# New instruction orders for five engines, eight warm pairs instead of ten, and the last half added and stored in two pieces

## The chip, the cores and the metric

One core of one Trainium2 chip runs the whole program. The metric is the device time of an execution in microseconds. The engines are TensorE (PE), VectorE (DVE), ScalarE (ACT), GpSimd (POOL) and SyncE (SP, which here only issues DMAs). SBUF is the on-chip memory that engines and DMA share; PSUM holds what PE writes.

## What is computed

Two layers of self-attention over the 32 x 32 pixels of 4 images with 128 channels, the second on the output of the first:

```python
n = h * w
xf = x.reshape(b, c, n)
q = jnp.einsum('rc,bcn->brn', Wq, xf) + bq[None, :, None]
k = jnp.einsum('rc,bcn->brn', Wk, xf) + bk[None, :, None]
v = jnp.einsum('oc,bcn->bon', Wv, xf) + bv[None, :, None]
energy = jnp.einsum('bri,brj->bij', q, k)
attn = jax.nn.softmax(energy, axis=2)
out = jnp.einsum('bcj,bij->bci', v, attn).reshape(b, c, h, w)
return gamma * out + x
```

Here b = 4, c = 128, n = 1024 and q, k have 16 rows. The second layer has other weights and the same form.

## The kernel before

There are 8 stages: 0 to 3 are the images in layer 0, 4 to 7 the same images in layer 1, so stage s + 4 needs the output x of stage s. Each stage works on 8 row tiles of 128 pixels. PSUM has a ring of three buffers [128 x 1024] and `out_psum` for the output. In a stage, by the names that the orders use:

- `QX`, `QK`: PE projects q and k in two steps (L630 to L643). `evac` (ACT) then `mask`, `stack` (POOL) do this for stage 1, `mask`, `stack` on DVE for stages 2 to 7 (L525 to L539): they add the bias and round to fp32r with a remainder, packed into `qk`. For stage 0 it is `raw` (L618): PE writes ring 0 and ring 1, ACT evacuates `qk_raw` and DVE `swapped_raw` in halves of 512 columns, and POOL stacks qk of stage 0 from `qk_raw` (L422 to L428). Energies of stage 0 use `qk_raw` and `swapped_raw`; tile i needs both halves of `qk_raw`, and only the first half of `swapped_raw` if i < 4 (L665, L666).
- `swap`: SP issues two DMAs that exchange the halves of `qk` into `qk_swapped` (L320 to L324).
- `E.s.i.r`: PE makes the energies of tile i in ring buffer r. `max` (DVE, L561) takes the negative row maximum, `sum` (ACT, L469) the row sums of exp, `log` (ACT) their logarithm.
- `parts` (POOL, L391 to L396), `shift` (PE), `rows` (DVE, L572) and `place` (SP, L326 to L336) bring maximum and logarithm as two extra rows into `qk`, so that
- `ET.s.k.r`: the transposed energies come out already shifted, and `attn` (ACT, L484) is exp of them. Before `attn` of stage s may overwrite tile k, the `lo` of tile k of the stage before must be done (or, for tiles 0 and 7, its product).
- `hi.s.k` and `lo.s.k`: tiles 1 to 6 of attn are cut in two fp32r numbers, `attn_hi` = rounded attn and `attn_lo` = attn - attn_hi. Tiles 0 and 7 are multiplied as fp32 and not cut. A `hi` is done by POOL (L359) or ACT (L490), a `lo` by POOL (L364) or DVE (L558). `v32` (DVE, L548), `v_hi` (POOL L370 or ACT L495) and `v_lo` (POOL L376 or DVE L553) do the same for v.
- `PH`: products of attn_hi with v_hi and v_lo (L741). `PV`: the product of attn_lo with v_hi, or for tiles 0 and 7 attn with v in fp32 (L747 to L752). They accumulate in `out_psum`.
- `finish.s.h` (DVE, L575): x plus gamma times the product, for one half of 512 columns. In stages 6 and 7 (`WHOLE`) a half is complete in one bank and takes one instruction (L586); elsewhere two. `store` (SP, L338) writes a half of layer 1's output to DRAM.

What runs when is written out by hand: `PE_ORDER`, `ACT_ORDER`, `DVE_ORDER`, `POOL_ORDER` and `SP_ORDER` (L51 to L113) list the pieces of each engine, with the loops over them at L589, L761 and their like. An engine takes its list strictly in order, and waits on semaphores for what each piece reads or overwrites. Which engine has a `hi`, `lo`, `v_hi` or `v_lo` is decided by the list in which it stands. `warm.0.n` in PE's order is n pairs of matmuls on a tile of zeros (`keep_warm`, L754), and `WARM_UP` = 10 such pairs run ahead of everything, as soon as POOL has cleared the zeros (L759, L760). Their results are not used.

At the start SP issues all loads: `weights` first (L310), then the two halves of x of stage 0 (L313), and the rest.

Of the kernel before, what the change touches and what calls it, by code (L numbers as in the profile page):

```python
# [832 lines left out]
```

## Time and profile before

| | us |
|---|---|
| median of 3 runs | 193.52 |
| lowest and highest of them | 192.95, 193.8 |
| the profiled execution | 193.06 |
| its span, from the first to the last instruction | 191.3 |
| busy in the span: PE, POOL, ACT | 179.1, 156.9, 155.5 |
| busy in the span: DVE | 145.7 |

The profile is one execution taken by the hardware profiler. A share of busy time over the whole span is a mean over a start, a long middle part and a tail, which have different limits, so the same numbers are better read by stretch. The chain that ended last is followed back from the last instruction to what released each one; it tells which engine was waited for, and in which part. Of a wait for several semaphores the profile names the one that came last.

### The profile page before, as it was taken

The numbers are of one execution on the slowest core, as the hardware profiler recorded it, in microseconds if no ns is written. First come the engines' busy times: TensorE is split into PE (matmuls) and PEld (weight loads), VectorE is DVE, ScalarE is ACT, GpSimd is POOL, SyncE is SP. The second block draws the span as 40 slices with busy tenths as digits, with TensorE's granted clock in tenths as the row PEclk, the third lists the DMA queues.
The fourth block names the chain that finished last, engine by engine and source line by source line (L and its number), as shares of the span: only waits on it lengthen the run. The fifth ranks groups of instructions, "written<-read, shape, count | busy, mean of one in ns | idle before, by whom it ended". The sixth has DMA issues, their size and how long they took to land.

```text
span 191.3 us, 3482 instructions
## 1 busy us (share of the span) xinstructions
PE 179.1 (94%) x1282; PEld 123.1 (64%) x1282; DVE 145.7 (76%) x137; ACT 155.5 (81%) x223; POOL 156.9 (82%) x120
## 2 busy tenths in 40 slices
...
GB/s 155 345 104 0 215 9 42 69 3 3 2 113 0 5 111 3 0 3 3 110 3 0 3 55 58 2 3 107 61 55 7 55 0 58 3 0 55 55 55 55
DMA packets 3890, 9.51 MB, mean 50 GB/s; under 512 B 548, under 2 KB 932, under 8 KB 3876
## 3 DMA queue, kind: packets, MB, share of 16 engines
...
## 4 chain that ended last, share of the span: by engine, by line
PE 34%; POOL 31%; ACT 15%; issue 10%; DMA 4%; DVE 4%; SPq 1%; POOLq 0%; DVEq 0%; ACTq 0%
POOL attn_lo L364 14%; PE out_psum L720 10%; POOL attn_hi L359 9%; ACT ring L472 8%; PE out_psum L722 7%; ACT attn L484 4%; DMA qk_swapped<-qk 4%; PE ring L671 3%; PE ring L697 3%; PE out_psum L756 3%; PE ring L642 2%; DVE neg_max L563 2%; PE ring L624 2%; PE ring L657 2%; ACT attn_hi L490 2%
## 5 line engine op out<-in xcount | busy, mean ns | idle before, releaser
L364 POOL TENSOR_TENSOR attn_lo<-attn,attn_hi 128x1024 fp32r<-128x1024 f32 x37 | 90.4, 2455 | 1.8 <-ACT attn_hi L490 1.3
L563 DVE TENSOR_REDUCE neg_max<-ring 128x1 f32<-128x1024 f32 x64 | 75.6, 1219 | 15.7 <-PE ring L673 15.3
L472 ACT ACTIVATE ring<-ring,neg_max 128x1024 f32<-128x1024 f32 x64 | 69.6, 1087 | 9.9 <-DVE neg_max L563 9.3
L484 ACT ACTIVATE attn<-ring 128x1024 f32<-128x1024 f32 x64 | 63.3, 1024 | 9.8 <-DVE attn_lo L558 5.6
L359 POOL TENSOR_SCALAR attn_hi<-attn 128x1024 fp32r<-128x1024 f32 x35 | 39.2, 1134 | 5.5 <-ACT attn L484 5.4
L699 PE MATMUL ring<-qk_swapped,qk 64*128 64x512 f32 x64 | 29.0, 478 | 0.0
L697 PE MATMUL ring<-qk,qk_swapped 64*128 64x512 f32 x64 | 28.5, 468 | 0.3
L671 PE MATMUL ring<-qk_swapped,qk 64*128 64x512 f32 x56 | 25.1, 452 | 3.4 <-ACT attn L484 1.7
L673 PE MATMUL ring<-qk,qk_swapped 64*128 64x512 f32 x56 | 25.7, 461 | 0.0
L558 DVE TENSOR_TENSOR attn_lo<-attn,attn_hi 128x1024 fp32r<-128x1024 f32 x11 | 19.4, 1778 | 5.5 <-POOL attn_hi L359 4.7
L723 PE MATMUL out_psum<-attn_hi,v_hi 64*128 64x512 f32 x72 | 23.0, 399 | 0.0
L722 PE MATMUL out_psum<-attn_hi,v_hi 64*128 64x512 f32 x72 | 23.0, 398 | 0.0
L723 PE MATMUL out_psum<-attn,v 64*128 64x512 f32 x48 | 22.6, 590 | 0.0
L722 PE MATMUL out_psum<-attn,v 64*128 64x512 f32 x48 | 22.6, 590 | 0.0
L722 PE MATMUL out_psum<-attn_hi,v_lo 64*128 64x512 f32 x72 | 22.2, 388 | 0.0
L723 PE MATMUL out_psum<-attn_hi,v_lo 64*128 64x512 f32 x72 | 22.2, 388 | 0.0
L722 PE MATMUL out_psum<-attn_lo,v_hi 64*128 64x512 f32 x72 | 20.9, 392 | 0.1
L723 PE MATMUL out_psum<-attn_lo,v_hi 64*128 64x512 f32 x72 | 20.9, 392 | 0.0
L697 PEld LDWEIGHTS ring<-qk,qk_swapped 64*128 64x128 f32 x64 | 11.5, 184 | 10.9 <-issue 9.9
L657 PEld LDWEIGHTS ring<-late,x_all 64*128 64x128 f32 x256 | 16.6, 187 | 2.5 <-issue 1.7
L671 PEld LDWEIGHTS ring<-qk_swapped,qk 64*128 64x128 f32 x56 | 10.3, 184 | 12.3 <-issue 10.3
L657 PE MATMUL ring<-late,x_all 64*128 64x128 f32 x256 | 17.6, 275 | 0.2 <-ACT ring L472 0.2
...
## 6 DMA issues: line engine op xcount, KB each, us to landing
qk_swapped<-qk SPq DMA_DIRECT2D x16, 256.0 KB, 3.7
out_dram<-x_all SPq DMA_DIRECT2D x8, 256.0 KB, 2.0
...
x_all<-x_in SPq DMA_DIRECT2D x2, 256.0 KB, 3.0
...
weights<-weights_in SPq DMA_DIRECT2D x1, 131.0 KB, 2.2
qk<-shift_rows SPq DMA_DIRECT2D x7, 8.0 KB
```

What stands on the lines that cost most here:

```text
L359: nc.gpsimd.tensor_scalar(attn_hi[:, k - 1], attn[:, k], 1.0, 0.0, ALU.mult, ALU.add).then_inc(cut_made["hi", "gpsimd"], 1)
L364: nc.gpsimd.tensor_tensor(attn_lo[:, k - 1], attn[:, k], attn_hi[:, k - 1].bitcast(fp32), ALU.subtract).then_inc(cut_made["lo", "gpsimd"], 1)
L472: nc.scalar.activation(e[:], e[:], ACT.Exp, bias=neg_max[s][:, i:i + 1], accum_out=row_sum[s][:, i:i + 1]).then_inc(sum_made, 1)
L484: nc.scalar.activation(attn[:, k], ring_tile("ET", s, k)[:].rearrange("p (a n) -> p a n", a=2), ACT.Exp).then_inc(attn_made, 1)
L563: nc.vector.tensor_reduce(neg_max[s][:, i:i + 1], ring_tile("E", s, i)[:], axis=AX.X, op=ALU.max, negate=True).then_inc(max_made, 1)
L657: last = nc.tensor.matmul(to[:, chunk], x_all[rows, s, chunk], late[rows, WV + layer(s)], start=step == 0 and j == 0, stop=step == 1 and j ...
L671: nc.tensor.matmul(to[:, 0:HALF], q_over_k[0:64, rows], k_over_q[0:64, 0:HALF], start=True, stop=True)
L673: nc.tensor.matmul(to[:, HALF:N], k_over_q[64:128, rows], q_over_k[64:128, HALF:N], start=True, stop=True).then_inc(e_mm, 1)
L697: nc.tensor.matmul(to[:, 0:HALF], k_over_q[0:64, first], q_over_k[0:64, part], start=True, stop=not added(s, h))
L699: last = nc.tensor.matmul(to[:, HALF:N], q_over_k[64:128, second], k_over_q[64:128, part], start=True, stop=not added(s, h))
L722: nc.tensor.matmul(out_psum[:, 0:HALF], v[0:64], a[0:64], start=start, stop=stop)
L723: last = nc.tensor.matmul(out_psum[:, HALF:N], v[64:128], a[64:128], start=start, stop=stop)
```

## The change

1. All five orders are new. The same pieces are computed, 64 `E`, 64 `ET`, 48 `PH`, 64 `PV` and so on. What changes hands: POOL has 33 `lo` instead of 37 and DVE 15 instead of 11; POOL has 34 `hi` instead of 35 and ACT 14 instead of 13; POOL has 4 `v_lo` instead of 5 and DVE 4 instead of 3; POOL has 5 `v_hi` instead of 3 and ACT 3 instead of 5. DVE's `lo` are now 0, 1, 3, 0, 1, 1, 5 and 4 in stages 0 to 7, where they were 0, 1, 1, 0, 1, 1, 4 and 3. POOL's `hi` are now 5, 5, 5, 4, 5, 4, 3 and 3, where they were 5, 5, 5, 4, 3, 6, 4 and 3. POOL's `v_hi` are now of stages 0, 1, 3, 4 and 6, where they were of 1, 3 and 5; its `v_lo` of 0, 1, 2 and 7, where they were of 0, 1, 2, 4 and 5.
2. `WARM_UP` is 8. The pairs within PE's order are 19 instead of 18.
3. `weights` is loaded by ACT's queue, ahead of ACT's table load; SP starts with x.
4. SP swaps stage 0 before stage 1.
5. The last `finish` (7.1) is two instructions of 256 columns with a semaphore of their own, and its store two DMAs.

```diff
-HALF = N // 2
+HALF, QUARTER = N // 2, N // 4
...
-WARM_UP = 10
+WARM_UP = 8
...
 PE_ORDER = """
-raw.0.0.0 raw.0.1.1 E.0.6.2 QX.1.0.0 E.0.0.1 QK.1.0.0 E.0.7.2 warm.0.2 E.0.4.0 E.0.2.1 E.0.1.2 warm.0.2 E.0.3.0
...
+raw.0.0.0 raw.0.1.1 warm.0.1 E.0.1.2 QX.1.0.0 E.0.2.1 QK.1.0.0 E.0.0.2 warm.0.2 E.0.7.0 E.0.3.1 E.0.5.2 warm.0.2
...
 SP_ORDER = """
-swap.1.0 swap.0.0 place.0.0 swap.2.0 place.0.1 place.1.1 swap.3.0 place.2.1 swap.4.0 place.3.1 swap.5.0 place.4.1
+swap.0.0 swap.1.0 place.0.0 swap.2.0 place.0.1 place.1.1 swap.3.0 place.2.1 swap.4.0 place.3.1 swap.5.0 place.4.1
...
+LAST = [use[1:3] for use in DVE_USES if use[0] == "finish"][-1]
...
         @block.sync
         def _(sp):
-            sp.dma_start(weights[:], weights_in).then_inc(weights_loaded, 16)
...
             def store(s, h):
+                if (s, h) == LAST:
+                    for q in range(2):
+                        part = slice(h * HALF + q * QUARTER, h * HALF + (q + 1) * QUARTER)
+                        sp.wait_ge(last_made, q + 1)
+                        sp.dma_start(out[s - B, :, part], x_all[:, s, part]).then_inc(stored, 16)
+                    return
...
-            sp.wait_ge(stored, 32 * B)
+            sp.wait_ge(stored, 32 * B + 16)
...
         @block.scalar
         def _(act):
+            act.dma_start(weights[:], weights_in).then_inc(weights_loaded, 16)
             act.preload_act_table_set("natural_log_exp_and_others")
...
+                if (s, h) == LAST:
+                    for q in range(2):
+                        part = slice(h * HALF + q * QUARTER, h * HALF + (q + 1) * QUARTER)
+                        nc.vector.scalar_tensor_tensor(out=x_all[:, s, part], in0=out_psum[:, part], scalar=gamma,
+                                                       in1=x_all[:, s, part], op0=ALU.mult, op1=ALU.add
+                                                       ).then_inc(last_made, 1)
+                    return
```

How the orders come out on the engines is shown at three places; the line numbers of the changed kernel are up to 17 higher. First PE, just behind the last matmul of the raw projection. The two instructions into a ring buffer from `swapped_raw` and `qk_raw` are one energy tile, those from `x_all` and `weights` the steps QX and QK of stage 1. Before:

```order
L624 MATMUL ring1<-x_all,weights 128x512
L671 MATMUL ring2<-swapped_raw,qk_raw 128x512
L673 MATMUL ring2<-qk_raw,swapped_raw 128x512
L642 MATMUL ring0<-x_all,weights 128x512 x2
L671 MATMUL ring1<-swapped_raw,qk_raw 128x512
L673 MATMUL ring1<-qk_raw,swapped_raw 128x512
```

After:

```order
L641 MATMUL ring1<-x_all,weights 128x512
L773 MATMUL out_psum<-zeros 128x512
L774 MATMUL out_psum<-zeros 128x512
L688 MATMUL ring2<-swapped_raw,qk_raw 128x512
L690 MATMUL ring2<-qk_raw,swapped_raw 128x512
L659 MATMUL ring0<-x_all,weights 128x512 x2
L688 MATMUL ring1<-swapped_raw,qk_raw 128x512
```

A warm pair has come in, and the sequence of forms is otherwise the same; the tiles are E.0.1 and E.0.2 where they were E.0.6 and E.0.0.

Second DVE, from `v32` of stage 3 to the end of stage 2's first `finish`. Before:

```order
L548 TENSOR_TENSOR v32_1<-ring2,late 128x1024
L558 TENSOR_TENSOR attn_lo<-attn,attn_hi 128x1024
L572 CAST shift_rows1<-ring0 16x128
L563 TENSOR_REDUCE neg_max4<-ring1 128x1
L563 TENSOR_REDUCE neg_max4<-ring0 128x1
L563 TENSOR_REDUCE neg_max4<-ring2 128x1
L563 TENSOR_REDUCE neg_max4<-ring1 128x1
L581 SCALAR_TENSOR_TENSOR x_all<-out_psum,weights,x_all 128x512
```

After:

```order
L558 TENSOR_TENSOR v32_1<-ring1,late 128x1024
L568 TENSOR_TENSOR attn_lo<-attn,attn_hi 128x1024
L582 CAST shift_rows1<-ring2 16x128
L568 TENSOR_TENSOR attn_lo<-attn,attn_hi 128x1024
L573 TENSOR_REDUCE neg_max4<-ring2 128x1
L540 TENSOR_SCALAR masked_hi<-ring0,weights 128x1024
L573 TENSOR_REDUCE neg_max4<-ring1 128x1
L547 SCALAR_TENSOR_TENSOR qk2<-ring0,weights,masked_hi 128x1024
L568 TENSOR_TENSOR attn_lo<-attn,attn_hi 128x1024
L598 SCALAR_TENSOR_TENSOR x_all<-out_psum,weights,x_all 128x512
```

DVE has three `lo` here where it had one, and mask and stack of stage 5 stand ahead of the `finish` instead of behind it, with fewer maxima.

Third POOL, from the last `parts` to its end. Before:

```order
L391 TENSOR_TENSOR shift7<-neg_max7,log_sum7 128x8
L394 TENSOR_SCALAR shift_parts7<-shift7 128x8
L396 TENSOR_TENSOR shift_parts7<-shift7,shift_parts7 128x8
L364 TENSOR_TENSOR attn_lo<-attn,attn_hi 128x1024
L359 TENSOR_SCALAR attn_hi<-attn 128x1024
L364 TENSOR_TENSOR attn_lo<-attn,attn_hi 128x1024
L359 TENSOR_SCALAR attn_hi<-attn 128x1024
L364 TENSOR_TENSOR attn_lo<-attn,attn_hi 128x1024
```

After:

```order
L400 TENSOR_TENSOR shift7<-neg_max7,log_sum7 128x8
L403 TENSOR_SCALAR shift_parts7<-shift7 128x8
L405 TENSOR_TENSOR shift_parts7<-shift7,shift_parts7 128x8
L385 TENSOR_TENSOR v_lo1<-v32_1,v_hi1 128x768
L368 TENSOR_SCALAR attn_hi<-attn 128x1024 x3
L373 TENSOR_TENSOR attn_lo<-attn,attn_hi 128x1024
L368 TENSOR_SCALAR attn_hi<-attn 128x1024
L373 TENSOR_TENSOR attn_lo<-attn,attn_hi 128x1024
```

Behind the last `parts` POOL had five `lo` and four `hi`; now it has `v_lo` of stage 7, four `hi` and two `lo`. `hi.6.3`, which stood second there, is in ACT's order now.

## Rows read from the trace of the kernel before

**Rows 1.** Busy us and instructions by stretch; then clock, DMA share, GB/s.

```profile
core 0: us, PE busy (x) PEld busy (x) DVE busy (x) ACT busy (x) POOL busy (x), PEclk, DMA share, GB/s
12.00:23.00 11.00, 10.31 (x61) 4.17 (x58) 8.80 (x8) 9.84 (x17) 4.46 (x5) 1.00 0.30 73
40.00:140.00 100.00, 96.80 (x787) 72.25 (x785) 85.85 (x84) 94.56 (x138) 98.26 (x70) 1.00 0.12 31
...
158.70:188.10 29.40, 28.13 (x112) 17.82 (x110) 18.48 (x15) 16.61 (x20) 20.72 (x13) 1.00 0.10 36
```

**Rows 2.** The chain that ended last, from the page, by engine.

```profile
PE 34%; POOL 31%; ACT 15%; issue 10%; DMA 4%; DVE 4%; SPq 1%; POOLq 0%; DVEq 0%; ACTq 0%
```

**Rows 3.** Timeline of the start: start us, us, instruction, [idle before <- releaser].

```profile
1.19 0.89 SPq L313 DMA_DIRECT2D x_all<-x_in  x2
...
1.31 0.60 PE L756 MATMUL out_psum<-zeros 64*128 64x512 bf16 x1 [1.31 <-POOL zeros L354]
...
4.70 0.54 PE L756 MATMUL out_psum<-zeros 64*128 64x512 bf16 x1
...
5.08 0.38 PE L756 MATMUL out_psum<-zeros 64*128 64x512 bf16 x1
...
5.38 3.70 PE L624 MATMUL ring<-x_all,weights 128*128 128x512 f32 x8
...
8.27 0.69 ACT L458 ACTIVATE qk_raw<-ring,weights 128x512 f32<-128x512 f32 x1 [0.96 <-PE ring L624]
...
10.02 0.66 PE L671 MATMUL ring<-swapped_raw,qk_raw 64*128 64x512 f32 x1 [0.94 <-DVE swapped_raw L519]
...
14.73 0.38 PE L756 MATMUL out_psum<-zeros 64*128 64x512 bf16 x1
...
14.95 0.38 PE L756 MATMUL out_psum<-zeros 64*128 64x512 bf16 x1
```

**Rows 4.** DMA issues, from the page: count, KB each, median us to landing.

```profile
out_dram<-x_all SPq DMA_DIRECT2D x8, 256.0 KB, 2.0
...
x_all<-x_in SPq DMA_DIRECT2D x2, 256.0 KB, 3.0
...
weights<-weights_in SPq DMA_DIRECT2D x1, 131.0 KB, 2.2
```

**Rows 5.** Two pieces of the chain that ended last: start us, us.

```profile
13.76 1.12 ACT unstacked L466
...
23.02 0.49 PE ring L671
```

**Rows 6.** Group of v_lo on POOL: busy us, mean ns, idle before.

```profile
L376 POOL TENSOR_TENSOR v_lo<-v,v_hi 128x768 fp32r<-128x768 f32 x5 | 9.1, 1826 | 0.0
```

**Rows 7.** Timeline rows of POOL and DVE in the middle.

```profile
82.74 2.37 POOL L364 TENSOR_TENSOR attn_lo<-attn,attn_hi 128x1024 fp32r<-128x1024 f32 x1
85.08 0.84 POOL L370 TENSOR_SCALAR v_hi<-v 128x768 fp32r<-128x768 f32 x1
...
123.70 1.43 DVE L558 TENSOR_TENSOR attn_lo<-attn,attn_hi 128x1024 fp32r<-128x1024 f32 x1
...
124.01 1.81 POOL L370 TENSOR_SCALAR v_hi<-v 128x768 fp32r<-128x768 f32 x1
```

**Rows 8.** Timeline rows from 160 to 170 us.

```profile
160.21 1.21 DVE L558 TENSOR_TENSOR attn_lo<-attn,attn_hi 128x1024 fp32r<-128x1024 f32 x1
...
162.66 2.84 DVE L558 TENSOR_TENSOR attn_lo<-attn,attn_hi 128x1024 fp32r<-128x1024 f32 x1
...
164.38 2.02 POOL L359 TENSOR_SCALAR attn_hi<-attn 128x1024 fp32r<-128x1024 f32 x1
...
166.55 0.70 PE L720 MATMUL out_psum<-attn_hi,v_hi 128*128 128x512 f32 x2 [1.20 <-POOL attn_hi L359]
...
169.93 1.03 ACT L484 ACTIVATE attn<-ring 128x1024 f32<-128x1024 f32 x1 [5.56 <-DVE attn_lo L558]
```

**Rows 9.** Timeline rows of the end.

```profile
188.07 0.75 DVE L586 SCALAR_TENSOR_TENSOR x_all<-out_psum,weights,x_all 128x512 f32<-128x512 f32 x1 [4.14 <-PE out_psum L720]
...
188.85 0.33 SPq L341 DMA_DIRECT2D out_dram<-x_all  x1
```

More of the change, by code:

```diff
@@ L73 @@
+PV.6.2 PH.6.5 PH.6.4 ET.7.0.0 ET.7.4.1 ET.7.1.2 PV.6.4 PH.7.3 PV.6.5 ET.7.6.1 ET.7.5.0 PV.7.0 PH.7.1 PV.7.3 PH.7.2
+PH.7.5 PV.7.1 PV.7.2 PH.7.4 PH.7.6 PV.7.5 PV.7.4 PV.7.6 PV.7.7
 """
 ACT_ORDER = """
[L75 to L77 removed]
@@ L83 @@
[L83 to L86 removed]
+sum.0.1 evac.1.0 sum.0.2 sum.0.0 sum.0.7 sum.0.3 sum.0.5 sum.0.4 log.0.0 sum.0.6 sum.1.0 sum.1.6 sum.1.7 log.0.1
@@ L87 @@
+attn.7.4 attn.7.0 attn.7.1 attn.7.5 hi.7.5 hi.7.4 attn.7.6 hi.7.6
 """
 DVE_ORDER = """
-max.0.6 max.0.0 max.0.7 max.0.4 max.0.2 max.0.1 max.0.3 max.0.5 max.1.4 rows.0.0 v32.0.0 max.1.7 max.1.6 mask.2.0
-stack.2.0 max.1.5 max.1.0 max.1.2 rows.0.1 max.1.3 max.1.1 max.2.4 max.2.7 max.2.1 rows.1.1 v32.1.0 finish.0.0
-max.2.3 max.2.0 mask.3.0 stack.3.0 max.2.6 max.2.2 max.2.5 finish.0.1 v32.2.0 lo.1.1 max.3.0 rows.2.1 max.3.1
-max.3.2 mask.4.0 stack.4.0 finish.1.0 max.3.6 max.3.5 max.3.4 max.3.3 max.3.7 max.4.4 finish.1.1 v32.3.0 lo.2.2
@@ new lines @@
+lo.2.3 max.4.0 mask.5.0 max.4.6 stack.5.0 lo.2.6 finish.2.0 max.4.3 v_lo.3.0 max.4.4 max.4.1 max.4.7 max.5.5
+finish.2.1 max.4.5 v32.4.0 max.5.1 max.5.4 rows.4.1 max.5.7 max.5.3 finish.3.0 mask.6.0 stack.6.0 v_lo.4.0 max.5.6
+max.5.0 max.5.2 max.6.1 finish.3.1 lo.4.1 v32.5.0 rows.5.1 max.6.3 max.6.2 max.6.0 v_lo.5.0 max.6.6 finish.4.0
+mask.7.0 stack.7.0 max.6.7 max.6.5 max.6.4 finish.4.1 rows.6.1 v32.6.0 max.7.6 max.7.0 max.7.4 max.7.2 finish.5.0
+max.7.5 max.7.7 max.7.1 lo.6.2 lo.5.6 v_lo.6.0 finish.5.1 max.7.3 v32.7.0 lo.6.6 rows.7.1 lo.6.3 lo.6.5 lo.6.4
@@ L99 @@
+finish.6.0 finish.6.1 lo.7.1 lo.7.2 lo.7.5 lo.7.4 finish.7.0 finish.7.1
 """
 POOL_ORDER = """
-mask.1.0 stack.1.0 parts.0.0 parts.0.1 v_lo.0.0 hi.0.2 hi.0.3 hi.0.1 lo.0.2 lo.0.3 lo.0.1 parts.1.1 hi.0.6 lo.0.6
-v_hi.1.0 hi.0.4 v_lo.1.0 lo.0.5 lo.0.4 hi.1.2 hi.1.1 hi.1.3 lo.1.2 parts.2.1 lo.1.3 hi.1.6 hi.1.5 lo.1.6 lo.1.5
-hi.2.1 v_lo.2.0 lo.1.4 hi.2.3 hi.2.2 lo.2.3 parts.3.1 hi.2.4 lo.2.1 v_hi.3.0 lo.2.6 hi.2.5 lo.2.4 lo.2.5 hi.3.3
-hi.3.1 hi.3.2 lo.3.2 lo.3.3 parts.4.1 lo.3.1 hi.3.4 lo.3.4 lo.3.6 lo.3.5 hi.4.3 hi.4.2 v_lo.4.0 lo.4.3 hi.4.1
```

80 lines of the change are left out of this document (39 added, 41 removed).

## The prediction

> **What bounds the kernel now.** I read the busy time by stretch first. From 40 to 140 us GpSimd (POOL) is busy 98.26 of 100 us, the tensor engine (PE) 96.80, ScalarE (ACT) 94.56 and VectorE (DVE) 85.85 [rows 1]. So there is no single slow engine: POOL has 1.7 us free, ACT 5.4, DVE 14.2, and the PE figure has to be read with care, since the ends of matmuls are modelled. Then the chain that ended last: PE 34% and POOL 31% of it, with ACT at 15% [rows 2]. In order of time it is the start-up through the first stages (to 23 us), then POOL, then PE. For the last 29.4 us, 158.7 to 188.1, PE is busy 28.13 [rows 1], nearly all products of the last two stages. Three regimes follow, and I cost the change in each: a serial start, a stretch where POOL has hardly a gap, and a tail where PE works off its queue.
>
> I use E for energies, ET for transposed energies, hi and lo for the two parts of an attention tile, v_hi and v_lo for those of v, as the orders do.
>
> **The start.** Ten warm pairs are issued before the raw projection. The last pairs start at 4.27, 4.70 and 5.08 us and the projection at 5.38 [rows 3]. From 1.31 to 4.70 there are eight pairs, one in 0.42 us; between two pairs at 14.73 and 14.95 it is 0.22 us. 512 columns in 0.42 and in 0.22 us are the 1.2 and the 2.4 GHz level. The pair at 4.70 takes 0.38, between the two: if x us of it are at the low level, 1.2x + 2.4(0.38 - x) = 0.512 thousand columns gives x = 0.33, so the clock rose at about 5.03 us. The engine had then been working without a break since 1.31 us. Two pairs fewer let the projection begin at 4.70, of which 0.33 us pass at half pace: 0.68 - 0.17 = **0.5 us earlier**. That needs the first half of x by 4.70. Its transfer is now issued at 1.19 us and that form takes 3.0 us to land [rows 3, 4], so about 4.2; with weights moved to ACT's queue it is issued 0.45 us sooner. No cost there: the work of ACT that follows waits for the projection. The bound on the other side: if the clock did not rise until the projection was over, its 8 rows in 3.70 us [rows 3] would take about 3.4 us more. I take no such delay, because PE has no idle gap there with 8 pairs either.
>
> Next, the first energies. Now E.0.6 is first; it reads rows of the second half of swapped_raw, and PE idles 0.94 us for it until 10.02 [rows 3]. Afterwards E.0.1 is first: it needs both halves of qk_raw but only the first half of swapped_raw. qk_raw's second half is written from 8.27 for 0.69 us, so to 8.96 [rows 3]. E.0.1 can start at about 9.03 rather than 10.02, the extra warm pair (0.22 us) fitting in the gap. E.0.2 then needs ring 1, free at 9.87, and E.0.1 with QX.1 keep PE busy beyond that. So QX.1 and QK.1, which stand in the same places, come **1.0 us earlier**. These 1.0 and 0.5 go on whole through the chain evac, mask and stack, swap, first E of stage 1 (evac at 13.76, the E at 23.02) [rows 5], since each step there starts when the one before it ends. SP now issues swap.0 before swap.1; POOL makes qk of stage 0 before that of stage 1, so it delays nothing and takes a transfer out of the chain's way: a gain if anything, taken as 0. One more warm pair in all within the order, 0.22 us, falls among waits: 0. **Start: -1.5 us.**
>
> **The middle.** POOL's run without a gap begins with hi.0.2. Counted in the orders from there to the end of stage 5: POOL gives up two lo (stage 2), v_lo.4 and v_lo.5; the hi of stage 4 and 5 exchange two for two with ACT; v_hi.4 comes and v_hi.5 goes. A lo is 2.37, a v_lo 1.83 on average [rows 6, 7]: 2 x 2.37 + 2 x 1.83 = 8.4 us off. v_hi.0, now POOL's, lies before the run, where POOL is busy 4.46 of 11 us [rows 1]: nothing. parts.0.1, which was before the run, is now inside: +0.8.
>
> But the work goes to DVE, and that is not free for POOL. At 123.70 DVE starts a lo; the v_hi that POOL starts at 124.01 takes 1.81 us, where the same form takes 0.84 when DVE is not at such an instruction (85.08) [rows 7]. So POOL stood about 1.0 us for a DVE instruction with two SBUF operands. Four such more: +3.9. The Trainium skill has this as a rule (SBUF — State Buffer, "SBUF: two separate sides"): the two engines share one pair of ports, and whichever starts first keeps it for its whole instruction. The trace agrees, with 1.81 against 0.84. Another place (Perfetto Trace Analysis, "Optimizing Scalar/DVE Operations") says that moving operations between these two "might not help". By the rows it helps by 2.37 - 1.0 = 1.4 for a lo; by that rule it would be 0, which is the first rival below.
>
> POOL's stretch thus falls by 8.4 - 0.8 - 3.9 = 3.7 us. That is an upper bound on what arrives at the end: ACT has only 5.4 us free in the same 100 and PE 3.2 [rows 1], each partly start-up of instructions, and an order is followed strictly, so what POOL wins is partly handed to waits for ACT or PE. The lower bound is 0, with a loss possible (third rival). DVE has the room: 4 x 1.2 = 4.8 us more against 14.2 free. I choose **-2.2 us**, some 60%, nearer to the upper end because POOL's row of the middle shows that these orders can keep it fed while ACT is at 95%.
>
> **The tail.** In the last two stages POOL has one lo fewer in each, v_lo.7 and v_hi.6 more; DVE one more lo in each, without v_lo.7; ACT v_hi.6 less and one hi more in stage 6. The products are the same, and PE sets the end. So only waits of PE count. The one of size is at 166.55, 1.20 us for hi.6.3 on POOL, which took 2.02 us because DVE's lo.6.6 (162.66, itself 2.84 for want of the port) ran beside it; and DVE's lo.6.3 after it kept ACT waiting 5.56 us, until 169.93 [rows 8]. In the new order hi.6.3 is ACT's, behind attn.6.4, and no port can hold it. The 1.20 can vanish; the five lo of stage 6 on DVE can bring a wait like it, since each can lose 1.6 us (2.84 against the 1.21 at 160.21 [rows 8]) to a POOL instruction. Ends: -1.2 and +1; taken **-0.6 us**.
>
> **The last half.** Now one instruction of 0.75 us from 188.07, a store issued at 188.85, landed about 2.0 us later [rows 9]. Per 512 columns more DVE needs about 0.5 us (1.21 for 1024 [rows 8] against 0.75), so a piece of 256 columns is 0.5 us and the second ends 0.4 later: 0.15 us later than now. The second store's 0.33 us of issue is free to go at once, as the first was issued 0.4 before. It carries half the bytes. One bound is the landing of 131 KB of weights, 2.2 us; the other the gap between those and a half of x of twice the size, 3.0 - 2.2 = 0.8 us [rows 4]. So the end moves between +0.15 + 0.2 = +0.35 and 0.15 - 0.8 = -0.65. The nearest row is the store's own, alone on the queues where the loads are not, so I take 1.75 instead of 2.0 for it: **-0.1 us**.
>
> **Sum.** -1.5 - 2.2 - 0.6 - 0.1 = -4.4 us. The profiled execution took 193.06 us, of which 191.3 is span; that gives 188.7. The median of the runs shown is 0.46 higher, which would give 189.1. I put down 188.9.
>
> **Rivals.**
> First, the moves between POOL and DVE bring nothing: DVE's lock costs as much as POOL sheds, or PE and ACT, 3 and 5 us behind POOL, become the bound at once. Then the start and the last half stay: 193.06 - 1.6 = 191.5. For it: three engines above 94%. Against it: 1.0 us of blocking for 2.37 of work.
> Second, all of it arrives: -1.5 - 3.7 - 1.2 - 0.25 = -6.65, so 186.4. For it: every stretch is then limited by what was shortened. Against: ACT would have to run at over 98%.
> Third, slower: DVE becomes the engine waited for. Five more of its instructions want the port while POOL holds it; at the 1.6 us that lo.6.6 lost, that is 8.2 us of waiting, and row maxima stand behind them, for which ACT waits and with ACT the ring and PE. At half of that, +4.1 with the middle's gain gone: 193.06 - 1.6 + 4.1 = 195.6. It turns the sign once more than 1.6 of the 8.2 us reach ACT. Against it: DVE's 14.2 us of room, which lie between these maxima. A small variant is the clock: risen only after the projection, 3.4 us lost, with the gains about 192.
> Fourth, the change does less than it says: the order's pairs of lo and POOL instructions fall elsewhere in time than planned, and waits merely move. That ends at the first rival's time.
>
> **How the numbers follow.** Forecast (187.3 to 190.7) 0.50; first and fourth rival (190.7 to 192.6) 0.23; second (below 187.3) 0.15; third (above 192.6) 0.12. The range runs from 186.2, which leaves out the better half of the second, to 192.5, which takes in the first. A measurement of this kernel can tell about 0.5%, 1 us. Faster by more than that, below 192.55: 0.50 + 0.20 + 0.14 = 0.84; within 0.5%: 0.07, from the first rival's edge and the mildest third; slower 0.09.
>
> **What would show it.** The raw projection begins near 4.7 us and its matmuls keep 0.43 us a row after 5.0; the first E stands near 8.5 and the first E of stage 1 near 21.5. If these are late, the start is wrong. POOL's busy time over the run should fall by 7 or so with some gaps for ACT or PE; if the fall is there but the end of stage 5 is not earlier by more than the start gave, the first rival holds. DVE's lo and v_lo tell the third: a mean above 2 us, and ACT idle for neg_max over 10 us. PE's wait of 1.20 before PH.6.3 should be gone, and from the start of DVE's last step to the end of the span 2.9 to 3.3 us should pass (3.2 now).

## The result: 2.4% slower, and the profile after

| | before | changed |
|---|---|---|
| median of the runs of this comparison, us | 193.24 (4 runs, 192.73 to 193.80) | 198.13 (4 runs, 196.58 to 198.66) |
| ratio, with its 95% interval | | 1.0237 [1.0198, 1.0275] |
| profiled execution, us | 193.06 | 196.58 |
| its span | 191.3 | 194.5 |
| busy PE, POOL, ACT, DVE | 179.1, 156.9, 155.5, 145.7 | 180.7, 145.3, 156.9, 151.8 |

Medians here and below are of all executions of a kernel, and the ratios leave out the slow ones, more than 1.5% above the kernel's fastest (one of lo26, one of clear_new, two of slow_three), so differences between experiments are taken from the ratios (0.01 is 1.9 us).

The forecast was 188.9 us with a range to 192.5. The time came out 5.6 us above that range, on the other side of the kernel before. The moves themselves arrived: POOL is busy 11.6 us less, DVE 6.1 more. What they were to buy did not.

The busy time by stretch of the changed kernel, to be held against [rows 1] (the second stretch is the tail again, 3.1 us later, since the end lies later):

```profile
core 0: us, PE busy (x) PEld busy (x) DVE busy (x) ACT busy (x) POOL busy (x), PEclk, DMA share, GB/s
40.00:140.00 100.00, 93.91 (x735) 71.63 (x734) 89.78 (x84) 89.85 (x126) 90.45 (x67) 0.98 0.11 29
161.80:191.30 29.50, 28.85 (x128) 18.64 (x124) 15.10 (x17) 18.76 (x22) 14.13 (x11) 1.00 0.10 37
```

From 40 to 140 us PE works off 735 instructions where it worked off 787, ACT runs 126 instructions instead of 138. POOL, which had 1.7 us free, has 9.6. DVE alone is busier, 89.78 instead of 85.85. In the tail PE stands idle for 0.65 us of 29.5, half of the 1.27 before.

The chain that ended last, by engine, from the page, against [rows 2]:

```profile
PE 51%; POOL 21%; DVE 13%; issue 8%; ACT 6%; DVEq 0%; POOLq 0%; ACTq 0%
```

DVE's share of that chain went from 4 to 13%. Where, is told by the chain in order of time. The same stretch of it in the kernel before (start us, us, what):

```profile
85.08 0.84 POOL v_hi L370
85.91 2.33 POOL attn_lo L364
88.25 1.02 POOL attn_hi L359
```

and in the changed kernel (`issue` is time for which the chain names no wait; at both places DVE's own timeline has it at work, on the rest of `lo.2.3` and on `mask.5.0`):

```profile
80.88 0.74 DVE attn_lo L568
81.62 1.03 issue
82.65 1.20 DVE neg_max L573
83.85 1.18 issue
85.03 1.21 DVE neg_max L573
86.25 1.19 DVE qk L547
87.44 3.11 DVE attn_lo L568
90.55 0.67 DVE x_all L598
91.25 0.76 DVE x_all L603
```

Before, the path runs through POOL's `hi` and `lo` without DVE. Now it runs from 80.88 to 92.01 through DVE's own list: `lo.2.3`, two maxima, `stack.5.0`, `lo.2.6`, the two halves of finish 2, and only then PE. The timeline rows of DVE and POOL at that place (start us, us, instruction):

```profile
80.88 1.85 DVE L568 TENSOR_TENSOR attn_lo<-attn,attn_hi 128x1024 fp32r<-128x1024 f32 x1 [0.75 <-POOL attn_hi L368]
...
87.35 3.20 DVE L568 TENSOR_TENSOR attn_lo<-attn,attn_hi 128x1024 fp32r<-128x1024 f32 x1
90.47 0.74 DVE L598 SCALAR_TENSOR_TENSOR x_all<-out_psum,weights,x_all 128x512 f32<-128x512 f32 x1
...
93.05 2.58 DVE L563 TENSOR_TENSOR v_lo<-v,v_hi 128x768 fp32r<-128x768 f32 x1
```

```profile
87.07 2.40 POOL L373 TENSOR_TENSOR attn_lo<-attn,attn_hi 128x1024 fp32r<-128x1024 f32 x1
...
92.44 2.38 POOL L373 TENSOR_TENSOR attn_lo<-attn,attn_hi 128x1024 fp32r<-128x1024 f32 x1
99.19 1.05 POOL L368 TENSOR_SCALAR attn_hi<-attn 128x1024 fp32r<-128x1024 f32 x1 [4.38 <-PE out_psum L740]
```

POOL's `lo.2.4` starts at 87.07, DVE's `lo.2.6` at 87.35: it lasts 3.20 us instead of 1.21, to the end of POOL's plus its own time. Then POOL's next `lo` starts at 92.44 and DVE's `v_lo.3` at 93.05 takes 2.58 instead of 0.93. PE waits for the finish between them, and then POOL itself stands 4.38 us, since its next `hi` needs a slot that PE's products free. The saved POOL time is spent in that gap. PE's own row, and its clock around it:

```profile
92.10 0.47 PE L739 MATMUL out_psum<-attn_hi,v_hi 64*128 64x512 f32 x1 [1.55 <-DVE x_all L603]
```

```profile
94.00:95.00 1.00, 1.00 (x7) 0.98 (x7) 1.00 (x1) 0.37 (x2) 0.81 (x1) 0.50 0.00 0
97.00:98.00 1.00, 1.00 (x12) 1.00 (x10) 1.00 (x1) 1.00 (x2) 0.00 (x0) 1.00 0.00 0
```

After waits of 0.60 and 1.55 us, the granted clock is at 0.50, its 1.2 GHz level, for some 3 us in this execution: 7 products in a microsecond instead of 12.

To see where time is lost I followed how much of PE's list was worked off, each product weighted by its usual duration, and compared the moments at which both kernels had done the same amount. Minus is ahead of the kernel before, in us. The two kernels take their pieces in different orders, so a single mark can be off by some tenths, now and then by 1 us; large steps count.

| before is at | changed | changed, run again | only the start changed |
|---|---|---|---|
| 15.4 | -1.50 | -1.15 | -0.71 |
| 76.8 | -1.45 | -1.14 | -0.61 |
| 85.1 | +0.34 | +0.67 | -0.61 |
| 93.9 | +4.13 | +2.88 | -0.61 |
| 103.6 | +2.57 | +2.56 | -0.60 |
| 155.8 | +4.07 | +4.47 | -0.76 |
| 188.0 | +3.16 | +3.54 | -0.72 |

The start's lead is still there at 77 us (between, it reads 0.6 to 2.0), is lost between 77 and 94, where DVE's rows above lie, and a second piece is lost where before is at 120 to 132, from 2.6 to 4.1, about `v_lo.5` (129.75 in the changed kernel, 2.43 us instead of 0.93). After 156 some 0.9 comes back.

### The profile page after: what moved, and what is told of

The parts are those of the page before. It is cut to its first block, busy times and chain, and to the rows that moved or that the text cites. A ratio compares the mean times of both kernels' runs of the same rounds, so it can differ in the third digit from the quotient of the medians.

```text
span 194.5 us, 3480 instructions
## 1 busy us (share of the span) xinstructions
PE 180.7 (93%) x1280; PEld 125.8 (65%) x1280; DVE 151.8 (78%) x143; ACT 156.9 (81%) x222; POOL 145.3 (75%) x116
## 4 chain that ended last, share of the span: by engine, by line
PE 51%; POOL 21%; DVE 13%; issue 8%; ACT 6%; DVEq 0%; POOLq 0%; ACTq 0%
PE out_psum L739 16%; PE out_psum L737 11%; POOL attn_lo L373 11%; POOL attn_hi L368 6%; PE ring L688 5%; DVE neg_max L573 5%; ACT ring L482 4%; PE ring L714 4%; DVE attn_lo L568 4%; PE ring L674 3%; PE out_psum L740 3%; PE ring L659 3%; PE out_psum L773 2%; PE ring L641 2%; POOL v_lo L385 2%
## 5 line engine op out<-in xcount | busy, mean ns | idle before, releaser
L373 POOL TENSOR_TENSOR attn_lo<-attn,attn_hi 128x1024 fp32r<-128x1024 f32 x33 | 80.8, 2458 | 5.2 <-ACT attn_hi L500 4.4
L482 ACT ACTIVATE ring<-ring,neg_max 128x1024 f32<-128x1024 f32 x64 | 69.6, 1087 | 11.1 <-DVE neg_max L573 10.3
L368 POOL TENSOR_SCALAR attn_hi<-attn 128x1024 fp32r<-128x1024 f32 x34 | 37.9, 1127 | 14.8 <-ACT attn L494 10.4
L714 PE MATMUL ring<-qk,qk_swapped 64*128 64x512 f32 x64 | 27.7, 451 | 2.4 <-ACT attn L494 1.2
L739 PE MATMUL out_psum<-attn_hi,v_hi 64*128 64x512 f32 x72 | 23.7, 408 | 2.8 <-DVE x_all L603 1.6
L690 PE MATMUL ring<-qk,qk_swapped 64*128 64x512 f32 x56 | 25.7, 459 | 0.0
L568 DVE TENSOR_TENSOR attn_lo<-attn,attn_hi 128x1024 fp32r<-128x1024 f32 x15 | 21.3, 1449 | 4.2 <-ACT attn_hi L500 2.3
L740 PE MATMUL out_psum<-attn_hi,v_hi 64*128 64x512 f32 x72 | 23.8, 410 | 0.0
L740 PE MATMUL out_psum<-attn_hi,v_lo 64*128 64x512 f32 x72 | 22.7, 395 | 0.0
L739 PE MATMUL out_psum<-attn_hi,v_lo 64*128 64x512 f32 x72 | 22.7, 395 | 0.0
L739 PE MATMUL out_psum<-attn_lo,v_hi 64*128 64x512 f32 x72 | 22.2, 402 | 0.0
L740 PE MATMUL out_psum<-attn_lo,v_hi 64*128 64x512 f32 x72 | 22.2, 402 | 0.0
L714 PEld LDWEIGHTS ring<-qk,qk_swapped 64*128 64x128 f32 x64 | 11.6, 186 | 14.8 <-issue 12.6
L739 PEld LDWEIGHTS out_psum<-attn_hi,v_hi 64*128 64x128 f32 x72 | 12.9, 189 | 5.3 <-issue 4.8
```

The costliest lines, as they stand in the source:

```text
L368: nc.gpsimd.tensor_scalar(attn_hi[:, k - 1], attn[:, k], 1.0, 0.0, ALU.mult, ALU.add).then_inc(cut_made["hi", "gpsimd"], 1)
L373: nc.gpsimd.tensor_tensor(attn_lo[:, k - 1], attn[:, k], attn_hi[:, k - 1].bitcast(fp32), ALU.subtract).then_inc(cut_made["lo", "gpsimd"], 1)
L482: nc.scalar.activation(e[:], e[:], ACT.Exp, bias=neg_max[s][:, i:i + 1], accum_out=row_sum[s][:, i:i + 1]).then_inc(sum_made, 1)
L568: nc.vector.tensor_tensor(attn_lo[:, k - 1], attn[:, k], attn_hi[:, k - 1].bitcast(fp32), ALU.subtract).then_inc(cut_made["lo", "vector"], 1)
L714: nc.tensor.matmul(to[:, 0:HALF], k_over_q[0:64, first], q_over_k[0:64, part], start=True, stop=not added(s, h))
L739: nc.tensor.matmul(out_psum[:, 0:HALF], v[0:64], a[0:64], start=start, stop=stop)
```

## Experiments

All medians and ratios are against runs of the kernel before on the same chip.

**The changed kernel once more, and one and two `lo` moved within DVE's list.** First question: is the loss the two maxima and the finish queued behind `lo.2.3` and `lo.2.6`? `lo26` puts `lo.2.6` behind them, `lo26_23` also `lo.2.3`.

```diff
 DVE_ORDER, lo26 (lo26_23 also exchanges lo.2.3 and max.4.0)
-lo.2.3 max.4.0 mask.5.0 max.4.6 stack.5.0 lo.2.6 finish.2.0 max.4.3 v_lo.3.0 max.4.4
+lo.2.3 max.4.0 mask.5.0 max.4.6 stack.5.0 finish.2.0 max.4.3 lo.2.6 v_lo.3.0 max.4.4
```

> The changed kernel once more, unaltered. It took 196.58 to 198.66 us, with a granted clock of 1.000 in the slowest of its four executions and 0.991 in the fastest. Theory A (DVE's queue: max.4.0 stands behind lo.2.3 and finish.2.0 behind lo.2.6, and PE waits for both; between 75 and 98 us the profiled execution lost 5.6 us of PE work against the kernel before): the same two waits of PE, 1.2 us and 1.8 to 2 us, stand in this trace too. Theory B (the loss is the fall of TensorE's clock at 93 us, about 1.7 us, and what follows): a trace at a full clock is shorter than 194.5 us of span and has no loss in that stretch. The spread of the times tells how much the clock can explain: 196.5 to 198.7 by either.

> The changed kernel with one piece moved: DVE does lo.2.6 behind finish.2.0 and max.4.3 instead of ahead of finish.2.0. Theory A: finish.2.0 starts when its product is done (88.6 us in the trace) and not at 90.5, PE's idle time of 1.8 to 2 us ahead of PH.2.6 goes, the clock has no reason to fall there: 2 to 3.5 us less than the changed kernel, so 194 to 196 us. Theory B: the same, if the fall of the clock goes with the idle time, and nothing if it falls anyway. Rival C (the orders are slow all over, DVE being the bound at 78% busy): under 1 us less, the wait returns a little later.

> As the run with lo.2.6 moved, and lo.2.3 moved too, from ahead of max.4.0 to behind it. In the trace DVE idles 0.75 us for hi.2.3, then works 1.85 us on lo.2.3 while max.4.0 could start at about 81.6; it starts at 82.65, so sum.4.0 and with it ring 2 and ET.3.1 are late. Theory A: another 0.8 to 1.2 us less than with lo.2.6 alone, PE's wait of 1.2 us ahead of ET.3.1 gone. Rival C: no further gain, since hi.2.3 on POOL and what hangs on lo.2.3 (attn.3.3) set the pace.

Measured: again 196.90 us, ratio 1.0193 [1.0108, 1.0279]; lo26 197.96, 1.0206 [1.0128, 1.0283]; lo26_23 198.79, 1.0281 [1.0209, 1.0353]. The profiled execution of `again` had a granted clock of 1.000 and had lost 2.88 us at the place where the other had lost 4.13; ten microseconds on both had lost 2.6. And of the four executions of the comparison the one at 1.000 was the slowest (198.66 us), the one at 0.991 the fastest (196.58). So the clock's fall is absorbed and not the cause. In lo26 the wait before finish 2 is gone. At the 94 us mark the loss is 0.90 instead of 4.13, but it is 2.30 at the next mark and 4.09 at the end. Its DVE, POOL and PE rows there:

```profile
91.37 1.27 DVE L568 TENSOR_TENSOR attn_lo<-attn,attn_hi 128x1024 fp32r<-128x1024 f32 x1
92.56 3.15 DVE L563 TENSOR_TENSOR v_lo<-v,v_hi 128x768 fp32r<-128x768 f32 x1
```

```profile
91.54 3.36 POOL L373 TENSOR_TENSOR attn_lo<-attn,attn_hi 128x1024 fp32r<-128x1024 f32 x1
```

```profile
98.24 0.47 PE L688 MATMUL ring<-qk_swapped,qk 64*128 64x512 f32 x1 [2.52 <-ACT ring L482]
```

`lo.2.6` now comes first at the port and takes 1.27; POOL's `lo` is held and takes 3.36; `v_lo.3` behind it waits for POOL and takes 3.15; the maximum behind that is late, ACT waits for it, and PE for ACT, 2.52 us. The wait moved by one instruction. Moving within DVE's list does not repair it.

**The start alone, put into the kernel before** (with `weights` on ACT's queue and `swap.0` first, too), and then with ten warm pairs again.

```diff
-WARM_UP = 10
+WARM_UP = 8
...
-raw.0.0.0 raw.0.1.1 E.0.6.2 QX.1.0.0 E.0.0.1 QK.1.0.0 E.0.7.2 warm.0.2 E.0.4.0 E.0.2.1 E.0.1.2 warm.0.2
+raw.0.0.0 raw.0.1.1 warm.0.1 E.0.1.2 QX.1.0.0 E.0.0.1 QK.1.0.0 E.0.7.2 warm.0.2 E.0.4.0 E.0.2.1 E.0.6.2 warm.0.2
```

> The kernel before with the start of the changed one alone: 8 warm pairs ahead, weights loaded by ACT's queue, swap.0 ahead of swap.1, one warm pair more and E.0.1 in the place of E.0.6, all else as before. In the changed kernel's trace this start was 1.5 us ahead at 20 us. Theory: the order behind it passes that on, 1.0 to 1.5 us less than the kernel before, 191.8 to 192.4. Rival (what POOL or PE sets in the middle takes it back, as PE's lead in the changed kernel shrank from 1.8 to 0.6 us between 40 and 60 us): under 0.5 us less.

> The kernel with only the changed start, and ten warm pairs ahead as before instead of eight. With eight, the raw projection took 3.70, 3.97, 4.71, 4.41 and 4.32 us in five profiles, because TensorE's rise to 2.4 GHz came at different points of it; with ten it took 3.70 in the kernel before. Theory (the gain of the start is the new first tile, 1.0 us, and the two pairs fewer give 0 to 0.5 by chance): 191.9 to 192.5, no slower than 192.03 by more than 0.3 and with less spread. Rival (the two pairs carry half of the gain): 192.4 to 192.8.

Measured: start 192.03 us over 10 runs, ratio 0.9928 [0.9900, 0.9956]; start10 192.06 over 12, 0.9948 [0.9924, 0.9973]. The gain is real, 0.7% or 1.4 us, and comes through to the end. What the warm pairs give is not resolved: the two ratios differ by 0.0020, 0.4 us, with 0.7 us of uncertainty, which excludes neither nothing nor the 0.5 us of the forecast. The projection's row in start and in start10:

```profile
4.84 4.71 PE L623 MATMUL ring<-x_all,weights 128*128 128x512 f32 x8
```

```profile
5.42 3.70 PE L623 MATMUL ring<-x_all,weights 128*128 128x512 f32 x8
```

With eight pairs it begins 0.58 us earlier and here ends 0.43 later. (This late end is one reason why the table shows a lead of only 0.6 to 0.7 us for this execution, where the runs give 1.4.) In five profiled executions with eight pairs, those of the changed kernel, again, start, back and start_last, its eight rows took 3.70, 3.97, 4.71, 4.41 and 4.32 us, and the others lie between: TensorE rises to the 2.4 GHz level at a point that differs from execution to execution. The Trainium skill has that too (TensorE: Matmul & The Clock Gate, "Part 1: The HAM clock gate"): it calls the number of slow matmuls at a kernel's start run-variable. The rows agree, 3.70 to 4.71 for the same eight.

**The last half in two pieces, on top of the start.**

```diff
+                if (s, h) == LAST:
+                    for q in range(2):
+                        part = slice(h * HALF + q * QUARTER, h * HALF + (q + 1) * QUARTER)
+                        nc.vector.scalar_tensor_tensor(out=x_all[:, s, part], in0=out_psum[:, part], scalar=gamma,
...
```

> The kernel before with the changed start and the last half finished and stored in two pieces. The start alone took 0.72% (1.4 us) off, 192.03 against 193.74. In the changed kernel's profile 3.3 us pass from the start of DVE's last step to the end of the span where 3.2 did. Theory (the split moves the end by nothing that can be measured): the same as the start alone, 192.0, plus or minus 0.3. The forecast said -0.1, with +0.35 and -0.65 as bounds.

Measured: 191.95 us over 12 runs, 0.9930 [0.9904, 0.9957], against 0.9928 for the start alone. Nothing that can be told from zero, as forecast.

**The port taken away.** DVE's `lo` and `v_lo` become fills with zero of the same size (so the low parts that DVE makes are missing from the output): same order, same waits on semaphores, but no second operand in SBUF. Once in the changed kernel, once in the kernel before.

```diff
-                nc.vector.tensor_tensor(attn_lo[:, k - 1], attn[:, k], attn_hi[:, k - 1].bitcast(fp32),
-                                        ALU.subtract).then_inc(cut_made["lo", "vector"], 1)
+                nc.vector.memset(attn_lo[:, k - 1].bitcast(fp32), 0.0).then_inc(cut_made["lo", "vector"], 1)
```

> The changed kernel with the reads taken out of what DVE does for attn_lo and v_lo: each is a memset to zero in the same place of the order, with the same waits and the same columns written (so DVE's share of the low parts is left out of the output). No two SBUF operands are read, so nothing is held at the port. Theory A (collisions at the port in DVE's queue): DVE's 6.7 us of excess ahead of 158 us and POOL's 7.7 us go, and the kernel falls by 4 to 7 us, to 190 to 193. Theory O (the orders make engines wait, ports or no ports): under 2 us less, 195 to 197. A memset may also be shorter than the 1.21 us of the subtraction; its own row tells by how much, and the companion run has the same.

> The same replacement in the kernel before: its 14 two-operand instructions of DVE become memsets (their low parts are left out of the output). It has 1.5 us of DVE excess ahead of 158 us, 5.3 us behind it, and 9.9 us on POOL. Theory A: POOL's stretch without a gap loses its 5 stalls of about 1 us, so 2 to 4 us less, 190 to 192; and the new orders without the port are then as fast as the old ones or faster, by up to the 1.5 us of the start. Theory O: the new orders stay slower than the old by 2 us or more even without the port.

Measured: clear_new 190.43 us, 0.9827 [0.9775, 0.9878]; clear_old 189.56, 0.9817 [0.9775, 0.9858]. So the fills give back 7.9 us in the changed kernel and 3.5 in the kernel before. Some of that is no port: a fill is 0.91 or 0.70 us, an undisturbed `lo` or `v_lo` 1.21 or 0.93. The two windows from 40 to 140 us, clear_new first:

```profile
40.00:140.00 100.00, 95.97 (x782) 73.12 (x779) 85.91 (x87) 92.90 (x136) 87.91 (x68) 1.00 0.12 31
```

```profile
40.00:140.00 100.00, 97.44 (x798) 73.38 (x796) 84.85 (x85) 95.36 (x139) 96.02 (x74) 1.00 0.13 34
```

(Each is one execution; that of clear_new took 193.14 us, the longest of its four. In it a swap issued at 71.41 us took 5.07 us, where 3.4 is the median in the changed kernel, and PE waited 1.33 us for it.) PE is back at 782 instructions instead of 735. But note the second finding. Without the port the two kernels differ by 0.1%, with 1.3 us of uncertainty on either side, although the new one has a start worth 1.4. So even then the new orders bring none of the 2.2 us expected of the middle, with POOL idle 12 us in 100. Moving load from POOL to DVE, in these orders, was worth nothing even where neither holds the other. What taking it from POOL alone would be worth was not run.

**Which side of the port, DVE's or POOL's?** In the changed kernel I compared each `lo` and `v_lo` with its undisturbed 1.21 or 0.93 us. DVE loses 7.6 us in all, 6.7 of it ahead of 158 us; before it lost 6.8, but only 1.5 ahead of 158, the rest in the tail, where no one waits. POOL loses 8.1 us, before 9.9. The next two start from clear_new, where no one holds anyone, and put back the lengths of one side alone, by spare fills on that engine. slow_dve has 9 fills of 0.91 us on DVE at the six places where it lost most (so `lo.2.3` with its fill is 1.82, in the changed kernel 1.85; the 0.16 us of issue ahead of each fill come on top, and the six places together last 14.3 us, in the changed kernel 13.7); slow_pool has 13 of 0.52 on POOL at ten places. slow_three has only the first three of DVE's places, 5 fills.

```diff
+HELD = {("lo", 2, 3): 1, ("lo", 2, 6): 2, ("v_lo", 3, 0): 2, ("v_lo", 5, 0): 2, ("lo", 6, 2): 1, ("v_lo", 6, 0): 1}
...
+        def hold(engine, what, s, i, counts, columns):
+            for _n in range(counts.get((what, s, i), 0)):
...
+                engine.memset(held[:, n % 4, 0:columns], 0.0)
...
                 wait_for_cut(dve, "hi", s, k)
+                hold(nc.vector, "lo", s, k, HELD, N)
```

> As clear_new (DVE's low parts are memsets, so left out of the output, and no port is held), with DVE alone made slower where it lost time at the port in the changed kernel: ahead of lo.2.3, v_lo.6 and lo.6.2 one more memset of 0.9 us into a spare tile, ahead of lo.2.6, v_lo.3 and v_lo.5 two, some 8 us in all. POOL is never held. Theory A (what stands behind them in DVE's queue is what the others wait for): most of the 4 us between the changed kernel and the old one come back, 193 to 196 us. Theory P (POOL's stalls of about 1 us set the pace, not DVE's queue): within 1 us of clear_new, 189.5 to 191.5.

> As clear_new (DVE's low parts left out of the output, no port held), with POOL alone made slower where DVE held it in the changed kernel: memsets of about 0.5 us into a spare tile, two ahead of hi.2.3, hi.3.1 and parts.5.1, one ahead of parts.2.1, lo.2.5, lo.4.4, hi.6.1, lo.6.1, parts.7.1 and lo.7.6, 6 to 7 us in all. Theory P: most of the 4 us come back, 193 to 196. Theory A: POOL has gaps in the new orders (it is busy 88 of 100 us in clear_new) that take them up, within 1.5 us of clear_new, 189.5 to 192.

> As slow_dve (DVE's low parts left out of the output, no port held), with the added memsets only at lo.2.3, lo.2.6 and v_lo.3, some 4.2 us instead of some 7.5. If the stretch of 80 to 95 us makes the loss: 196 to 198, near slow_dve's 198.3. If each place adds its share: 193.5 to 195.5, about half way from clear_new's 190.4.

Measured: slow_dve 198.26 us, 1.0242 [1.0194, 1.0290]; slow_pool 191.27, 0.9898 [0.9852, 0.9944]; slow_three 193.99 over 10 runs, 1.0009 [0.9975, 1.0044]. Against clear_new, 8.2 us of fills on DVE (9.6 with their issue) lengthen the kernel by 8.0 us; 6.8 us of fills on POOL by 1.4; 4.6 us at DVE's first three places (5.3 with issue) by 3.5. Each has an uncertainty of 1.2 to 1.4 us from the two intervals, so the effect on POOL's side is hardly told from nothing. And 1.0242 is the changed kernel's 1.0237. The window from 40 to 140 us, slow_dve first, then slow_pool:

```profile
40.00:140.00 100.00, 94.09 (x736) 70.29 (x734) 88.28 (x91) 89.86 (x128) 86.44 (x65) 0.98 0.12 31
```

```profile
40.00:140.00 100.00, 97.61 (x796) 72.70 (x794) 86.32 (x89) 94.62 (x135) 93.22 (x80) 1.00 0.13 34
```

With DVE alone slowed PE works off 736 instructions there, in the changed kernel 735; with POOL alone slowed 796, more than the 787 of the kernel before. The chain that ended last in slow_dve, in the same stretch:

```profile
85.73 1.19 DVE qk L558
86.93 0.16 issue
87.09 0.91 DVE held L173
88.00 0.16 issue
88.16 0.91 DVE held L173
89.07 0.16 issue
89.23 0.91 DVE attn_lo L580
90.15 0.56 DVE x_all L609
...
91.58 0.47 PE out_psum L750
```

It is the chain of the changed kernel with the wait for the port replaced by plain work. It needs no port and no stall of POOL to give the same time: in these orders the cause is the length of DVE's list at these places. That the two times agree to 0.1 us is partly chance, since DVE's other low parts are 0.2 to 0.3 us shorter each as fills. That the place matters, and not the sum on DVE alone, is argued from the chain: no run put the same fills where nothing urgent stands behind them.

**Giving the load back to POOL.** Two `lo` of stage 2 (back), then also `v_lo.3` and `v_lo.5` (back_four), from DVE to POOL.

```diff
 POOL_ORDER
-v_lo.2.0 lo.1.5 hi.2.1 hi.2.2 parts.3.1 lo.2.1 hi.2.3 v_hi.3.0 lo.2.5 hi.2.6 hi.2.4 lo.2.4 hi.3.1
+v_lo.2.0 lo.1.5 hi.2.1 hi.2.2 parts.3.1 lo.2.1 hi.2.3 lo.2.3 v_hi.3.0 lo.2.5 hi.2.6 lo.2.6 hi.2.4 lo.2.4 hi.3.1
...
 back_four, besides
-lo.3.1 hi.3.5
+lo.3.1 v_lo.3.0 hi.3.5
-hi.5.3 lo.5.1
+hi.5.3 v_lo.5.0 lo.5.1
```

> The changed kernel with lo.2.3 and lo.2.6 given back to POOL (behind hi.2.3 and behind hi.2.6), so that DVE has one lo in stage 2 as before. It takes 2.4 to 3.2 us off DVE's queue between 80 and 91 us and puts 4.7 us on POOL's, where POOL stands idle 4.4 us from 94.8 on in the changed kernel. Theory A: finish.2.0 and max.4.0 are no longer held, PE loses less in 75 to 98 us: 2 to 4 us less than the changed kernel, 194 to 196. Theory O: no change or slower, POOL's 4.7 us come on top.

> The changed kernel with lo.2.3, lo.2.6, v_lo.3 and v_lo.5 on POOL instead of DVE, so all of the output is computed and DVE meets the port in the middle only at lo.1.1, lo.2.2, v_lo.4, lo.4.1, where it lost 0.3 us in all. POOL gets 8.4 us more work. If DVE's queue is the loss and POOL's gaps (it idles for 9.5 us of 40 to 140) can take the work: 193 to 195, 2 to 4 us less than the changed kernel. If POOL's load is as dear as DVE's waits: 196 or more, no better than back (196.3).

Measured: back 196.33 us, 1.0142 [1.0097, 1.0187]; back_four 197.21, 1.0188 [1.0134, 1.0241]. back gains 1 to 2 us, by which of the two runs of the changed kernel it is held against. In back_four DVE loses only 0.9 us at the port ahead of 158, and still it is no better than the changed kernel run again: taking the length off DVE by putting it on POOL does not bring the time back in the new orders. A row of PE in back_four:

```profile
107.27 0.20 PE L701 MATMUL ring<-units,shift_parts 64*16 64x64 f32 x2 [1.79 <-POOL shift_parts L405]
```

There POOL's list is the late one. With the four pieces on DVE its finish and maxima are late, with them on POOL `parts` is; that each list was laid out for the others is my reading of it.

**The tail's one wait, mended alone.** On top of start_last, `hi.6.3` goes from POOL to ACT.

```diff
 ACT_ORDER
-hi.6.6 hi.6.4 attn.6.3 attn.6.7 attn.7.3
+hi.6.6 hi.6.4 attn.6.3 attn.6.7 hi.6.3 attn.7.3
 POOL_ORDER
-lo.6.2 hi.6.3 lo.6.1 hi.7.3
+lo.6.2 lo.6.1 hi.7.3
```

> start_last (191.95 us) with hi.6.3 moved from POOL to ACT, behind attn.6.7, where ACT stands idle 5.6 us. In the old order POOL's hi.6.3 is held by DVE's lo.6.6, PE waits 1.2 us for it, and DVE's lo.6.3 comes late and is held in turn 2.2 us by lo.6.1, for which ACT waits 5.6 us. Theory (this chain sets the tail; without any port the tail of the old kernel shrank by 1.6 us): 0.8 to 1.6 us less, 190.3 to 191.2, faster than both kernels. Rival (PE's own work sets the tail, and the wait returns one tile later): 191.7 to 192.2.

Measured: 190.81 us (6 runs, 190.34 to 191.14), ratio 0.9865 [0.9834, 0.9895]; start_last is at 0.9930. The intervals do not overlap: 1.3 us by the one move (1.1 by the medians). It is **the fastest kernel of this study that computes the whole output**: 1.3% under the kernel before, 3.6% under the changed one (0.9865 / 1.0237 = 0.964). PE's wait of 1.20 us [rows 8] is gone, and of ACT's 5.56 us 3.64 are left:

```profile
167.81 1.03 ACT L492 ACTIVATE attn<-ring 128x1024 f32<-128x1024 f32 x1 [3.64 <-DVE attn_lo L566]
```

## Why the prediction was wrong, point by point

**The start, -1.5: right in size.** Alone it measured -1.4. The projection began at 4.76, the first energies at 8.62, the first of stage 1 at 21.31 (forecast 4.7, 8.5, 21.5):

```profile
4.76 3.70 PE L641 MATMUL ring<-x_all,weights 128*128 128x512 f32 x8
...
8.62 0.59 PE L688 MATMUL ring<-swapped_raw,qk_raw 64*128 64x512 f32 x1
...
21.31 0.49 PE L688 MATMUL ring<-qk_swapped,qk 64*128 64x512 f32 x1
```

Its split is open. The 0.5 of the warm pairs took one execution's moment of the clock's rise, 5.03 us, as a constant, which it is not; start against start10 gives 0.4, with 0.7 of uncertainty. The loads did not gain as assumed: x was issued 0.45 us sooner and took 3.5 us instead of 3.0, `weights` took 3.6 on ACT's queue, where it took 2.2 on SP's. PE waited for neither.

**The middle, -2.2 with bounds 0 and -3.7: this is the step that failed.** The whole change is +4.6 us; with -1.4 for the start, -1 for the tail and 0 for the last half, the middle is +7.0. Three sentences of the working fell.

"DVE has the room: 4 x 1.2 = 4.8 us more against 14.2 free." The 14.2 us are mostly short waits for PE's rings, one ahead of each maximum. They are no store that a piece of work can draw on at any place. An instruction put ahead of a maximum or a finish that PE waits for is on the path nearly whole: in slow_dve 9.6 us added to DVE's list, 8.2 of them busy, came out as 8.0 at the end. I had checked the share of busy time, not what stands behind each moved instruction.

"So POOL stood about 1.0 us for a DVE instruction ... Four such more: +3.9." The port was costed on POOL's side alone; DVE's wait for it stood at nothing in the sum. POOL's loss did not rise, it fell from 9.9 to 8.1. The new DVE instructions mostly came second at the port: DVE's loss ahead of 158 us went from 1.5 to 6.7 us. In these rows a DVE piece that came second behind POOL's `lo` waited up to 2.2 us (3.15 for 0.93), a POOL one behind DVE's about 1.0 (3.36 for 2.37).

"That is an upper bound on what arrives." POOL shed more than the 3.7 I wrote, it is idle 9.6 us of 100 instead of 1.7, and nothing of it arrived. clear_new shows that this is not the port alone: with no port held the new orders are still no faster. POOL without a gap [rows 1] had looked like the limit; the time it gained went into waits for PE (4.38 us in one piece) and for ACT.

**The tail, -0.6: right in mechanism, small in size.** The wait for `hi.6.3` vanished, and no wait like it came (the longest of PE there is 0.54 us, for `parts`). In the changed kernel 0.9 us comes back after 156; tail63, in the old orders, measures the move of `hi.6.3` by itself at 1.3 us. It was the optimistic end, -1.2, that was near.

**The last half, -0.1: right**, by start_last. From DVE's last start to the end of the span 3.3 us pass; 3.2 before. The two stores land in 1.9 us, hardly less than the 2.0 of twice the bytes:

```profile
191.23 0.88 DVE L591 SCALAR_TENSOR_TENSOR x_all<-out_psum,weights,x_all 128x256 f32<-128x256 f32 x2 [4.14 <-PE out_psum L737]
```

```profile
out_dram<-x_all SPq DMA_DIRECT2D x2, 128.0 KB, 1.9
```

**The rivals.** The third happened, DVE as the engine waited for, and it was rated at 0.12. Its mechanism was written down rightly: maxima queued behind, their lateness passed to ACT, ring and PE. Its price was too low: it took half of 8.2 us, 4.1, where slow_dve has most of such length arrive. With the 6.7 us that DVE lost ahead of the tail instead of 4.1 its sum would have given 198.2; that this meets the measured time is partly luck, since back_four, with 0.9 us of such loss, took 197.2. Of the two signs named for it one fails: the means of DVE's low parts are under 2 us (1.45 for a `lo`, 1.94 for a `v_lo`), since most are not held at all. The other, ACT idle over 10 us for the maxima, is met with 10.3, but tells little beside the 9.3 before. The row of the `lo`, whose mean hides the four held instructions that stand ahead of something urgent:

```profile
L568 DVE TENSOR_TENSOR attn_lo<-attn,attn_hi 128x1024 fp32r<-128x1024 f32 x15 | 21.3, 1449 | 4.2 <-ACT attn_hi L500 2.3
```

The rule of the Trainium skill that was weighed (SBUF — State Buffer, "SBUF: two separate sides": whichever of the two starts first holds the pair for its whole instruction) agrees with every row shown here, on both sides. What the forecast did with it was one-sided.

**Open.** That the length of DVE's list costs the time is shown by slow_dve, in the new orders and with nothing held at the port. The four moves alone, put into the old orders, were not run, so what they would cost there, and how much of the loss belongs to the other new orders, is not known; back_four, 1.9% slower with the four back on POOL, says that the new orders without them are slow too. Why the new middle brings nothing even with the port out of play (clear_new against clear_old) is not settled: with 1.4 us for the start, the two ratios put its loss at 1.6 us, with 1.3 of uncertainty. And which arrangement of these five orders would have kept POOL's relief was not found; four attempts at mending single places (lo26, lo26_23, back, back_four) brought at most 1 to 2 us.
